# Two-layer graph attention on one core: one pool of eight PSUM banks with a bank table, paired scores, and a new order on every engine

## The reference

```python
# layer 0
q, k, v = x @ Wq + bq, x @ Wk + bk, x @ Wv + bv        # 8 heads of 32
scores = where(adj == 0, -inf, q k^T / sqrt(32))
y = softmax(scores) v @ Wo + bo + x
x = layernorm(y) * gamma + beta
# layer 1
nx = layernorm(x) * ln1_g + ln1_b
scores = q(nx) k(nx)^T / sqrt(32) + where(adj > 0, 0.1 * adj * adj, -inf)
x1 = x + softmax(scores) v(nx) @ wo + bo
out = x1 + gelu((layernorm(x1) * ln2_g + ln2_b) @ w1 + b1) @ w2 + b2
```

## Time and profile before

| | |
|---|---|
| median of 3 runs | 2299.97 us (2299.87 to 2300.84) |
| the profiled execution's own time | 2303.0 us |
| its span | 2301.2 us |
| granted clock of PE, mean | 0.985 |
| PE busy | 2200.5 us, 96% |
| DVE busy | 2034.2 us, 88% |
| ACT busy | 1838.3 us, 80% |
| POOL busy | 1300.8 us, 57% |
| the 16 DMA engines | 10.3% |
| chain that ended last | PE 59%, DVE 19%, ACT 13%, issue 7% |

### The profile page before, as it was taken

The page is one execution under the profiler, slowest core; times in us unless marked ns, Lnnn a source line. Parts: engine busy times, 40 slices in busy tenths (PEclk is TensorE's granted clock), DMA queues, the critical chain, the costliest instruction groups (busy, mean ns, idle before and its releaser), DMA issues.

```text
span 2301.2 us, 58678 instructions
## 1 busy us (share of the span) xinstructions
PE 2200.5 (96%) x19008; PEld 1906.3 (83%) x19008; DVE 2034.2 (88%) x7173; ACT 1838.3 (80%) x5774; POOL 1300.8 (57%) x909
## 2 busy tenths in 40 slices
PE   6789999999999999999999999999999999999987
PEld 5678888888888888888888888888888888888776
DVE  5799999999999999999999999999999999999862
ACT  4688889888888888888888888888888888888862
POOL 2566565566566566556566656556656556556530
PEclk7999999999999999999999999999999999999988
DMA  4101101101100101100101110101110110110000
GB/s 126 35 22 38 33 21 32 36 27 36 32 23 27 36 27 36 32 27 24 36 27 36 33 35 14 36 29 35 36 32 14 36 36 27 36 32 6 24 10 19
DMA packets 80766, 72.77 MB, mean 32 GB/s; under 512 B 3008, under 2 KB 72256, under 8 KB 80704
## 3 DMA queue, kind: packets, MB, share of 16 engines
q1 hardware_dynamic: 80704, 71.98, 10.3%
HBM read 55.20 MB, written 16.78 MB: 31 GB/s over the span
## 4 chain that ended last, share of the span: by engine, by line
PE 59%; DVE 19%; ACT 13%; issue 7%; POOL 1%; DVEq 0%; DMA 0%; ACTq 0%; SPq 0%; POOLq 0%
PE ps_j L413 39%; PE ps_s L374 8%; PE ps_t L389 6%; DVE hl L821 4%; ACT pm L532 4%; DVE r L813 4%; ACT hh L603 3%; PE ps_j L424 3%; DVE pm L717 3%; PE ps_o L405 3%; ACT hf L609 2%; DVE hf L766 2%; ACT L603 2%; DVE stats L798 2%; DVE q1l L762 1%
## 5 line engine op out<-in xcount | busy, mean ns | idle before, releaser
L870 POOL TENSOR_TENSOR pm<-pm,rinv 128x512 f32<-128x512 f32 x512 | 559.8, 1109 | 633.6 <-DVE rinv L728 633.6
L532 ACT ACTIVATE pm<-pm,nmax 128x128 f32<-128x128 f32 x2048 | 794.1, 391 | 120.1 <-DVE nmax L717 116.6
L717 DVE CUSTOM_DVE_ANT_0 pm<-ps_s,m 128x128 f32<-128x128 f32 x2048 | 458.5, 285 | 68.8 <-PE ps_s L374 62.0
L532 ACT ACTIVATION_READ_ACCUMULATOR pm<-pm,nmax 128x1 f32 x2048 | 386.0, 188 | 0.0
L821 DVE TENSOR_TENSOR hl<-hf,hh 128x512 fp32r<-128x512 f32 x256 | 282.5, 1131 | 34.1 <-ACT hf L609 31.3
L389 PE MATMUL ps_t<-ident,pm 128*128 128x128 f32 x2048 | 286.3, 278 | 17.1 <-POOL pm L870 16.6
L413 PE MATMUL ps_j<-w2h,hh 128*128 128x256 f32 x1024 | 294.8, 288 | 5.7 <-DVE hl L821 5.7
L413 PE MATMUL ps_j<-w2h,hl 128*128 128x256 f32 x1024 | 287.8, 281 | 0.0
L413 PE MATMUL ps_j<-w2l,hh 128*128 128x256 f32 x1024 | 287.8, 281 | 0.0
L389 PEld LDWEIGHTS ps_t<-ident,pm 128*128 128x128 f32 x2048 | 232.5, 142 | 45.4 <-POOL pm L870 21.6
L885 POOL TENSOR_TENSOR rstd<-veps,power 128x4 f32<-128x4 f32 x96 | 98.0, 1021 | 279.6 <-DVE veps L806 276.5
(11 more groups left out here) (148 smaller groups left out, 6370.4 us busy)
## 6 DMA issues: line engine op xcount, KB each, us to landing
xTr<-in_xT SPq DMA_DIRECT2D x32, 512.0 KB, 3.7
xy<-in_x SPq DMA_DIRECT2D x32, 512.0 KB, 3.9
out<-x SPq DMA_DIRECT2D x32, 512.0 KB, 2.9
m<-in_adj SPq DMA_DIRECT2D x32, 256.0 KB, 2.8
a<-in_adj SPq DMA_DIRECT2D x32, 256.0 KB, 4.2
r<-in_wo SPq DMA_DIRECT2D x2, 256.0 KB, 5.9
x<-in_w SPq DMA_DIRECT2D x1, 512.0 KB, 8.7
v<-in_w SPq DMA_DIRECT2D x1, 512.0 KB, 7.2
```

The source lines that it names most:

```text
L532: last = nc.scalar.activation(pm[:, g % 2, h, :], pm[:, g % 2, h, :], ACT.Exp, bias=nmax[:, g % 2, h:h + 1], scale=-1.0, accum_out=rsum[:, ...
L717: last = nc.vector.tensor_tensor_reduce(out=pm[:, g % 2, h, :], in0=ps_s[c][:, j * N:(j + 1) * N], in1=m[:, g, :], scale=1.0, scalar=3e38, ...
L870: tt(pm[:, g % 2, hs, :], pm[:, g % 2, hs, :], rinv[:, g % 2, hs].rearrange("p (h a) -> p h a", a=1).to_broadcast([P, HC, N]), ALU.mult).t ...
```

## The change

- **One pool.** `ps_s`, `ps_t`, `ps_o` and `ps_j` become one list `ps` of eight banks. `JOBS` now lists 66 jobs of an iteration, scores (S0, S1), flips (F0, F1) and values (V0, V1) among them, each with how many batches it is behind and the bank it takes. `filled`, `taken` and `free_of` count uses of a bank; the old semaphores `scores_full`, `masked`, `pt_full`, `pt_a`, `pt_b`, `pv_done`, `ot_lo` are gone.
- **Scores side by side.** On PE, graphs 0 and 1 of a batch, and in layer 1 also graphs 2 and 3, are now next to each other; `flip` of the graph that used the same buffer of `pm` may then come behind the scores on PE.
- **A new wait.** `flipped` on DVE waits, with no operation, until PE has flipped the graph whose buffer of `pm` the next `mask_scores` overwrites. It stands eleven times in DVE's list.
- **New orders** on PE, ACT, DVE and POOL. The lists' cut has moved: PE's iteration begins with the WO1 job instead of MLP2.
- In the start, the small products for the biases share bank 1, and `second_products` waits for `bias_step` 5 ahead of its first product.

```diff
 JOBS = [
-    ("MLP2", 0, 3), ("QKV0", 4, 0), ("MLP2", 1, 3), ("QKV0", 5, 0), ("T1", 0, 1), ("WO1", 0, 2), ("T1", 1, 1),
+    ("WO1", 0, 3, 5), ("V1", 1, 3, 1), ("S0", 4, 1, 3), ("S0", 5, 1, 2), ("F0", 0, 1, 4), ("F0", 1, 1, 0),
...
-BANKS = 3
+BANKS = 8
...
-        ps_s = [bank("ps_s0"), bank("ps_s1")]
-        ps_t = [bank("ps_t0"), bank("ps_t1")]
-        ps_o = bank("ps_o")
-        ps_j = [bank(f"ps_j{n}") for n in range(BANKS)]
+        ps = [bank(f"ps{n}") for n in range(BANKS)]
...
             def second_products():
                 pe.wait_ge(mlp_loaded, 96)
+                pe.wait_ge(bias_step, 5)
...
             def scores(l, b, g):
...
-                    before = earlier(l, b, g, 1)
-                    if before:
-                        pe.wait_ge(masked[before[0]], 2 * slot(*before[1:]) + 2)
+                    outs = [open_job(b, f"S{l}", 2 * g + c) for c in (0, 1)]
...
             def flip(l, b, g, c):
                 if exists(b):
                     pe.wait_ge(norm_done[l], 2 * slot(b, g) + c + 1)
-                    before = earlier(l, b, g, 1)
-                    if before:
-                        pe.wait_ge((pt_a, pt_b)[c][before[0]], slot(*before[1:]) + 1)
+                    out = open_job(b, f"F{l}", 2 * g + c)
...
+            def flipped(l, b, g, c):
+                if exists(b):
+                    filled(dve, b, f"F{l}", 2 * g + c)
...
             def body(i):
...
+                out_proj(Y, i - 3, 0); values(Y, i - 3, 1); scores(X, i - 1, 2); flip(X, i - 1, 0, 0)
+                flip(X, i - 1, 0, 1); qkv(Y, i - 2, 0); out_proj(Y, i - 3, 1); qkv(Y, i - 2, 1); qkv(Y, i - 2, 2)
+                flip(X, i - 1, 1, 0); flip(X, i - 1, 1, 1); qkv(Y, i - 2, 3); scores(X, i - 1, 3); values(X, i - 1, 0)
+                qkv(Y, i - 2, 4); flip(X, i - 1, 2, 0); qkv(Y, i - 2, 5); flip_rows("T2", i - 3, 0)
+                flip_rows("T2", i - 3, 1); scores(Y, i - 2, 0); scores(Y, i - 2, 1); flip(X, i - 1, 2, 1)
+                flip(X, i - 1, 3, 0); flip(X, i - 1, 3, 1); mlp_up(i - 3, 0); mlp_up(i - 3, 1); mlp_up(i - 3, 2)
+                values(X, i - 1, 1); mlp_up(i - 3, 3); mlp_up(i - 3, 4); mlp_up(i - 3, 5); mlp_up(i - 3, 6)
+                mlp_up(i - 3, 7); out_proj(X, i - 1, 0); out_proj(X, i - 1, 1); qkv(X, i, 0); flip(Y, i - 2, 0, 0)
+                flip(Y, i - 2, 0, 1); scores(Y, i - 2, 2); scores(Y, i - 2, 3); mlp_down(i - 3, 0); qkv(X, i, 1)
+                flip(Y, i - 2, 1, 0); qkv(X, i, 2); flip(Y, i - 2, 1, 1); qkv(X, i, 3); qkv(X, i, 4)
+                mlp_down(i - 3, 1); mlp_down(i - 3, 2); values(Y, i - 2, 0); scores(X, i, 0); scores(X, i, 1)
+                flip(Y, i - 2, 2, 0); flip(Y, i - 2, 2, 1); mlp_down(i - 3, 3); flip(Y, i - 2, 3, 0); qkv(X, i, 5)
+                flip(Y, i - 2, 3, 1); flip_rows("T1", i - 1, 0); flip_rows("T1", i - 1, 1)
```

More of the change, by code:

```diff
@@ L47, in exists @@
     return 0 <= b < NB if isinstance(b, int) else True
[L50 to L53, removed]
+POS = {(name, n): at for at, (name, n, _, _) in enumerate(JOBS)}
+BEHIND = [job[2] for job in JOBS]
+BANK = [job[3] for job in JOBS]
 def uses_before(i, pos):
+    same = [q for q in range(len(JOBS)) if BANK[q] == BANK[pos]]
     def count(it):
-        same = range(pos % BANKS, len(JOBS), BANKS)
         n = sum(exists(k - BEHIND[q]) for k in range(FIRST, it) for q in same)
@@ L63, in uses_before @@
         return count(i)
-    return i * PER_BANK + (count(FIRST_FULL) - FIRST_FULL * PER_BANK)
+    return i * len(same) + (count(FIRST_FULL) - FIRST_FULL * len(same))
 def place(h):
@@ L323, in first_weights @@
                 pe.wait_ge(lo_made, 2 * C)
+            bias = ps[1]
             def shift_products():
@@ L840, in body @@
-                out_lo(Y, i - 2, 1); residual("WO1", i - 2, 0); mask_scores(X, i, 2, 0); recip(X, i, 1)
-                copy_pt(X, i, 0); mask_scores(X, i, 2, 1); residual("WO1", i - 2, 1); qk_lo(Y, i - 1, 0)
-                norm_stats(2, i - 2)
+                split_h(i - 3, 6); residual("WO0", i - 1, 1); split_h(i - 3, 7); norm_stats(0, i - 1)
+                copy_pt(Y, i - 2, 0); recip(Y, i - 2, 1); mask_scores(Y, i - 2, 2, 0); mask_scores(Y, i - 2, 2, 1)
+                qk_lo(X, i, 0); norm_rows(0, i - 1); flipped(Y, i - 2, 1, 0); mask_scores(Y, i - 2, 3, 0)
@@ new lines, in body @@
+                flipped(Y, i - 2, 1, 1); mask_scores(Y, i - 2, 3, 1); qk_lo(X, i, 1); qk_lo(X, i, 2)
+                copy_pt(Y, i - 2, 1); v_out(X, i, 0); qk_lo(X, i, 3); mask1(i - 1); recip(Y, i - 2, 2)
+                residual("MLP2", i - 3, 0); recip(Y, i - 2, 3); norm_stats(1, i - 1); out_lo(Y, i - 2, 0)
+                flipped(Y, i - 2, 2, 0); mask_scores(X, i, 0, 0); flipped(Y, i - 2, 2, 1); mask_scores(X, i, 0, 1)
+                norm_rows(1, i - 1); flipped(Y, i - 2, 3, 0); mask_scores(X, i, 1, 0); copy_pt(Y, i - 2, 2)
@@ new lines, in body @@
+                copy_pt(Y, i - 2, 3); recip(X, i, 0); flipped(Y, i - 2, 3, 1); mask_scores(X, i, 1, 1)
+                residual("MLP2", i - 3, 1); lo("T1", i - 1, 0); v_out(X, i, 1); lo("T1", i - 1, 1)
+                out_lo(Y, i - 2, 1); flipped(X, i, 0, 0); mask_scores(X, i, 2, 0); recip(X, i, 1); copy_pt(X, i, 0)
+                residual("WO1", i - 2, 0); flipped(X, i, 0, 1); mask_scores(X, i, 2, 1); residual("WO1", i - 2, 1)
+                qk_lo(Y, i - 1, 0); norm_stats(2, i - 2); copy_pt(X, i, 1); recip(X, i, 2); qk_lo(Y, i - 1, 1)
@@ new lines, in body @@
+                qk_lo(Y, i - 1, 2); mask_scores(X, i, 3, 0); mask_scores(X, i, 3, 1); qk_lo(Y, i - 1, 3)
+                norm_rows(2, i - 2); v_out(Y, i - 1, 0); recip(X, i, 3); v_out(Y, i - 1, 1); lo("T2", i - 2, 0)
+                mask_scores(Y, i - 1, 0, 0); lo("T2", i - 2, 1); out_lo(X, i, 0); flipped(X, i, 2, 1)
+                mask_scores(Y, i - 1, 0, 1); copy_pt(X, i, 2); copy_pt(X, i, 3); flipped(X, i, 3, 0)
+                mask_scores(Y, i - 1, 1, 0); flipped(X, i, 3, 1); mask_scores(Y, i - 1, 1, 1); mask0(i + 1)
@@ L844, in _ @@
+                split_h(i - 2, 0); split_h(i - 2, 1); split_h(i - 2, 2); recip(Y, i - 1, 0); out_lo(X, i, 1)
+                split_h(i - 2, 3); split_h(i - 2, 4); split_h(i - 2, 5); x_lo(i + 1, 0); x_lo(i + 1, 1)
+                residual("WO0", i, 0)
             iterate(dve, body, {FIRST: first_weights})
```

175 lines of the change are left out of this document (66 added, 109 removed), and 14 rows, old and new, of the table JOBS.

## The result

The change made the kernel slower: 2320.82 us median (2319.48 to 2322.51) against 2300.4 (2299.87 to 2301.09), ratio 1.0089, 95% interval 1.0071 to 1.0106. The forecast was 2279, range 2238 to 2309. The profiled execution took 2319.48 us, span 2317.7.

What follows compares the result with a forecast made beforehand. PE, busy 96% of the span, was taken as the bound: 68.65 - 1.17 (shape changes) - 1.48 (old waits) + 1.96 (T2's wait) = 67.96 us an iteration. Times 31 that is 21.4 us less: 2279 us, range 2238 to 2309.

Steps and rivals of the forecast that it cites:

- Waits elsewhere: Other waits, such as T1, layer 0's graph 3 flips and the first MLP1 job: no added cost.
- Scores side by side: On PE, six fewer changes of product shape at 0.195 us each: 1.17 us an iteration less, bounds 0 and 1.56.
- WO0: PE's wait ahead of WO0 for the bank held by ACT's gelu: counted gone, 0.39 us an iteration less.
- T2: PE's wait ahead of the T2 transposes for DVE's norm rows: grows from 1.09 to 1.96 us, way 12.39 us.
- The flipped waits: DVE's eleven new waits for PE's flips: costed at nothing; without their margin of a few tenths, 0.88 us comes back.
- Start and end: The time outside the 31 steps, 173 us before: change taken as 0, +-8 us.
- the clock: Waits bring PE's 1.2 GHz level for a tenth of each iteration: 211 us more, 2490 us; chance 0.03.
- A second wait behind T2: DVE late by 0.6 us for layer 0's last flip: 19 us on top, 2297 us, no change; chance 0.11.
- The wait at T2 stays short: `normalise` falls behind the last norm row: wait 1.23 us, iteration 67.23, 2256 us; without POOL beside, 2218; chance 0.17.
- The way does not shorten: The way to T2 stays 13.36 us, the wait becomes 2.93, iteration 68.93, 2309 us; chance 0.10.
- pairs save nothing: Opening two banks costs what a shape change costs, the 1.17 stays: iteration 69.13, 2315 us; chance 0.05.
- the signs named for wrong: Step over 0.2 between paired scores; PE wait elsewhere as long as T2's; late second WO1 residual; clock under 1.00.

Runs made afterwards that it cites:

- run 5: The change with 24 instructions that only count put ahead of DVE's first wait, loops unaltered: 2286.66 us, ratio 0.9936.
- run 7: Run 1's kernel with POOL's `normalise(X, i, 2, 1)` put back ahead of both `pad_k`: 2260.72 us, ratio 0.983.
- run 9: Run 1's kernel with DVE's `recip(Y, i - 2, 2)` put ahead of `mask1` instead of behind it: 2283.26 us, ratio 0.9932.
- run 1: The change with semaphores counted in a stride of 16 per iteration for every bank, DVE's loop body 308 instructions instead of 322: 2284.87 us, ratio 0.9933.
- run 8: Run 1's kernel with DVE's `norm_rows(2)` moved ahead of `recip(X, i, 2)`: 2249.25 us, ratio 0.9778.
- run 11: Run 1's kernel with `norm_rows(2)` moved to just behind `recip(X, i, 2)`, and run 9's move besides: 2267.83 us, ratio 0.9857.
- run 13: Run 8's kernel with banks 0 and 3 exchanged in the table from entry F0 4 on: 2249.77 us, ratio 0.978.
- run 14: Run 13's kernel with run 9's move of the reciprocal too: 2248.71 us, ratio 0.9768.
- run 15: Run 14's kernel with `qk_lo(Y, i - 1, 3)` between the two masks of graph 3 instead of behind them: 2233.67 us, ratio 0.9718.
- run 16: Run 14's kernel with `qk_lo(Y, i - 1, 3)` ahead of both masks of graph 3: 2257.46 us, ratio 0.981.
- run 6: The kernel before the change with 70 instructions that only count ahead of DVE's first wait: 2377.87 us, ratio 1.0339.
- run 10: Run 1's kernel with `mlp_down(i - 3, 0)` put between the paired `scores(Y, i - 2, 2)` and `scores(Y, i - 2, 3)`: 2303.67 us, ratio 1.0013.
- run 2: Run 1's kernel with 14 instructions that only count added to DVE's loop body, 322 again: 2288.0 us, ratio 0.9942.

## Why the prediction was wrong

The step that failed is one that the prediction's sum does not have. It counts operations and waits on data, and DVE's loop cut, 0.34 us of "issue" in the kernel before, has no term. In the change it became 2.0 us, and 0.8 more three steps on, ahead of `norm_stats`, because the loop body landed where it must be fetched anew. "Waits elsewhere", costed at nothing, had no margin for that: the masks of graph 2 came late, and PE waited for their bank ahead of `flip(Y, i - 2, 1, 0)`, 0.66 us an iteration from start to start, and 0.2 in scores near it. The clock stretches, all at T2, cost another 5 x 1.7 / 20 = 0.4. Together 1.3 us, which is 69.66 less run 5's 68.32 (the clock's part is an estimate: five stretches of 3.4 us at half speed, in the 20 iterations); over 26 turns of the loop 34 us, the distance of the medians. With the loop in its place the change takes 2286.7 us, 0.64% faster than before, inside the range; 14 us less where 21 were forecast.

Term by term, by run 5's profile unless said:

- *Scores side by side*, 1.17 us less: right. The second scores job starts 0.81 us after the first, with no excess, and a pair taken apart costs 0.4. PE without its two waits needs 68.32 - 1.95 - 0.51 = 65.86 us, for which 66.00 stood.
- *WO0*, gone: right. It starts 1.40 us behind the last MLP1 job, as the MLP1 jobs do among themselves.
- *T2*, 1.96 us of wait: right, 1.95 from start to start (3.46 against 1.51). The way from the job behind WO1 to T2 is 1130.57 - 1118.14 = 12.43 us in the changed kernel, for 12.39, and its parts are right too. The second residual starts 0.20 us into it, for 0.2, and ACT is not waited for behind it (the next DVE step starts at 1118.94). The rows grew by 0.45 (3.22 to 3.67); run 7 splits that into 0.27 less and 0.72 more, for 0.28 and 0.73.

```profile
1118.14 0.40 PE L395 MATMUL ps<-acth,wqkv1h 128*128 128x512 f32 x1
1118.34 0.69 DVE L773 TENSOR_TENSOR x<-ps,r 128x512 f32<-128x512 f32 x1
1130.57 0.66 PE L406 MATMUL ps<-ident,r 128*128 128x128 f32 x4 [1.81 <-DVE r L801]
```

- *The flipped waits*, nothing: right for PE. DVE idles 24.4 / 20 = 1.2 us an iteration at them, time that it has.
- *Waits elsewhere*, nothing: wrong by 0.51 also where the loop lies well. `mask1` takes 5.6 us beside `pad_k` and `shift_y0` (3.4 before), the reciprocal of graph 2 stands behind it, and the second half of that graph's flip starts 1.00 us behind the first instead of 0.49. Run 9 took back 0.19 an iteration; there POOL's `pad_k`, which stands ahead of the `normalise`, holds the rest.
- *Start and end*, nothing, +-8: 2285.7 - 31 x 68.32 = 168 us for 173; right.

Of the rivals, *the clock* came true in small, seven stretches instead of a tenth of each iteration, and helped to make the sign wrong. Going through eight banks is not by itself what brings them: runs 1 and 8 use the same table and have none. *A second wait behind T2* is absent in the change, and is not what the cures of T2 met either: in runs 8 and 11 PE waits ahead of T2, at `flip(X, i - 1, 2, 0)`, and in runs 13 and 14 behind it, but at `scores(Y, i - 2, 0)`, for `pad_k`. *The wait at T2 stays short* did not happen in the change; in run 7, with the `normalise` out of the way of the rows, it is 1.24 us for the rival's 1.23. Without the wait, in runs 8, 11 and 13 to 16, the kernel takes 2234 to 2268 us, not the 2218 that the sum without waits gave. *The way does not shorten* and *pairs save nothing* are refuted. Of the signs named for wrong one was there, a granted clock under 1.00. PE waits at other jobs were there too, but about half as long as T2's at the longest (0.9 against 1.8 us), so that sign, as it is worded, was not; no sign asked for DVE's cut.

## What to carry to other kernels

A change that alters the number of instructions, register and wait instructions included, also moves every loop body in the code, and that alone was worth 1.5% (the change against run 5) and 3.4% (run 6) here. So look at the instruction queue's packets in the page, and at idle times that end in "issue" at a loop's cut, before any other explanation; if they appear, shift the loop by some instructions that do nothing and time it again. And a wait on a tight way is not a sum to be collected: of what one step gave up, nearly half in run 8, three quarters in run 11 and all in run 13 was waited for at the next. So read what stands second in line before the first is removed.

## What the runs showed of the hardware

- A DVE loop of 307 to 322 instructions runs without instruction packets where it touches three pieces of 128, and with five packets of 8 KB a turn where it touches four; DVE then idles 2.0 us (the change) and 3.0 us (run 6) at the cut in the mean. 24 instructions moved the change from one to the other.
- Single stretches of 3.4 us at the 1.2 GHz level came in the steady part of four kernels (7 in the change, 9 in run 6, 3 in run 9, 6 in run 10, between 400 and 2050 us), all with a PE wait of up to 1.8 us an iteration at T2; 23 of these 25 begin within 1 us of the T2 transposes. Runs 1, 2 and 5 had that wait and no stretch; no kernel without it had one.
- Four norm rows of DVE took 1.38 us with no POOL operation beside them, 2.09 beside one `normalise`, 2.95 beside a `pad_k`, and 3.67 beside a `pad_k` and a `normalise`.
